# Layer 0's pass by source in a four-layer graph network: the one-hot of a batch made by one comparison on VectorE

## The reference, cut to what matters

```python
# edge_index = stack([src, dst]); row, col = src, dst;  h = relu(layernorm(x))
messages = h[col] * fsum                       # fsum: one number for each edge, from edge_weight
agg = jax.ops.segment_sum(messages, row, num_segments=x.shape[0])
out = softplus(agg @ Wi1 + bi1) @ Wi2 + bi2
out = gamma * (out - mov_mean) * rsqrt(mov_var + 1e-3) + beta
x = x + out
```

## Time and profile before

| | us |
|---|---|
| median of three runs | 8948.55 |
| lowest and highest run | 8941.01, 8954.63 |
| the profiled execution | 9018.93 |
| its span from first to last instruction | 9017.2 |
| VectorE busy in the span | 3871.8 (43%) |
| GpSimd busy | 5604.4 (62%) |
| ScalarE busy | 1730.6 (19%) |
| TensorE matmuls busy | 3603.3 (40%) |
| mean granted TensorE clock | 0.611 |

### The profile page before, as it was taken

The page is one execution under the profiler, slowest core; times in us unless marked ns, Lnnn a source line. Parts: engine busy times, 40 slices in busy tenths (PEclk is TensorE's granted clock), DMA queues, the critical chain, the costliest instruction groups (busy, mean ns, idle before and its releaser), DMA issues. The chain is left out here.

```text
span 9017.2 us, 92622 instructions
## 1 busy us (share of the span) xinstructions
PE 3603.3 (40%) x19869; PEld 3184.5 (35%) x19870; DVE 3871.8 (43%) x10252; ACT 1730.6 (19%) x2818; POOL 5604.4 (62%) x5253
## 2 busy tenths in 40 slices
PE   4000001344435734444434444426666665344433
PEld 1000001333335633333323333325565654333333
DVE  8886001222225644434464434463333336444445
ACT  3000000000004721111121111122111114111111
POOL 2788777666666456666646666645666661666665
PEclk9555555666667955555555555556666667566666
DMA  5233333222224411111221111122222231121113
GB/s 188 62 81 92 90 89 89 66 68 68 67 67 135 127 44 42 42 42 42 41 32 42 42 42 42 42 24 71 65 64 64 64 64 23 45 45 44 44 44 46
DMA packets 385196, 561.62 MB, mean 62 GB/s; under 512 B 206364, under 2 KB 242692, under 8 KB 385000
## 3 DMA queue, kind: packets, MB, share of 16 engines
q0 software_dynamic: 171520, 305.19, 15.5%
q1 hardware_dynamic: 213608, 255.67, 9.1%
HBM read 374.00 MB, written 189.03 MB: 62 GB/s over the span
## 5 line engine op out<-in xcount | busy, mean ns | idle before, releaser
L1307 POOL DMA_INDIRECT edge_buf<-node_table,ixr x1664 | 1694.1, 1018 | 1044.6 <-PEq L1040 491.7
L1307 POOL DMA_INDIRECT Y<-node_table,ixr x1664 | 1665.1, 1001 | 936.8 <-issue 492.9
L1461 PE MATMUL bank<-ident_b,Y 128*128 128x128 bf16 x2520 | 325.5, 310 | 2303.3 <-ACT Y L1423 2253.6
L409 POOL DMA_INDIRECT edge_records<-edge_buf x800 | 991.0, 1239 | 252.6 <-issue 249.5
L1203 POOL DMA_INDIRECT layer_messages<-edge_buf,ixr x832 | 869.9, 1046 | 424.4 <-issue 253.4
L1461 PEld LDWEIGHTS bank<-ident_b,Y 128*128 128x128 bf16 x2520 | 242.4, 140 | 2380.7 <-ACT Y L1423 2328.6
L1036 PE MATMUL bank<-edge_buf,Y 128*128 128x129 f32 (+2 forms) x3744 | 843.9, 400 | 13.6 <-DVE H L1057 13.6
L1057 DVE TENSOR_TENSOR ACC<-ACC,bank 128x129 f32 (+2 forms) x2080 | 604.5, 291 | 505.9 <-PE bank L1036 260.8
L1012 DVE TENSOR_TENSOR Y<-iota_row,dloc 128x1024 f32<-128x1024 f32 x420 | 516.5, 1230 | 700.6 <-PEq L1040 651.5
L1036 PE MATMUL bank<-Y 128*128 128x129 f32 (+1 forms) x3328 | 797.6, 418 | 0.5 <-DVE ACC L1057 0.3
L1397 DVE TENSOR_REDUCE pk<-bank 128x16 f32<-128x48 f32 (+1 forms) x312 | 101.2, 324 | 1564.5 <-remote 1285.3
(11 more groups left out here) (280 smaller groups left out, 5728.5 us busy)
## 6 DMA issues: line engine op xcount, KB each, us to landing
edge_buf<-edge_records SPq DMA_DIRECT2D x208, 288.0 KB
layer_messages<-ACC SPq DMA_DIRECT2D x26, 2112.0 KB
XI<-layer_messages SPq DMA_DIRECT2D x78, 528.0 KB, 3.5
edge_records<-H SPq DMA_DIRECT2D x1, 29952.0 KB
edge_buf<-node_table,ixr POOLq DMA_INDIRECT x1664
Y<-node_table,ixr POOLq DMA_INDIRECT x1664
edge_buf<-in_edge_attr_dram SPq DMA_DIRECT2D x50, 500.0 KB
edge_buf<-layer_messages SPq DMA_DIRECT2D x26, 528.0 KB, 3.5
```

The lines of the kernel that those rows point to most:

```text
L409: pool.indirect_dma_start(rec_d, bass.IndirectOffsetOnAxis(ap=ixs[h][:, j:j + 1], axis=0), rec[h][:, j, :], None).then_inc(scattered[h], 16)
L1307: pool.indirect_dma_start(ring[q][:, j, 0:w], None, table, bass.IndirectOffsetOnAxis(ap=ixr[q][:, j:j + 1], axis=0)).then_inc(rows_in[q], 16)
L1461: ins = nc.tensor.transpose(tb_[:, j * P:(j + 1) * P], ohb[h][:, j * P:(j + 1) * P], ident_b[:, :])
```

## The change

The three steps on GpSimd and ScalarE go. VectorE makes the one-hot in one instruction, a comparison of two broadcast operands with `is_equal`. In VectorE's order the comparison for batch q + 2 stands before the additions of batch q, and two of them stand ahead of all. The wait for a free one-hot buffer and the wait for the batch's rows move from GpSimd to VectorE with it. VectorE's rounds are now written out for the first and for the last one, with a hardware loop of 11 between them. The semaphores `apart` and `distance` go. SyncE and TensorE keep their programs.

```diff
-            msg_in, apart, distance, oh_ready, used = ([sem(f"{n}{q}") for q in range(deep)] for n in
-                                                       ("msg_in", "apart", "distance", "oh_ready", "used"))
+            msg_in, oh_ready, used = ([sem(f"{n}{q}") for q in range(deep)] for n in ("msg_in", "oh_ready", "used"))
...
-                @block.gpsimd
-                def _(pool):
-                    def body(i, first):
-                        for q in range(deep):
-
-                            if q >= oh_deep:
-                                pool.wait_ge(used[q - oh_deep], i + 1)
-                                pool.sem_inc(poolt, 1)
-                            elif not first:
-                                pool.wait_ge(used[q + deep - oh_deep], i)
-                                pool.sem_inc(poolt, 1)
-                            pool.wait_ge(msg_in[q], i * 16 + 16)
-                            pool.sem_inc(poolt, 1)
-                            nc.gpsimd.tensor_tensor(onehots[q], iota_row[:, :].unsqueeze(1).to_broadcast([P, G, P]),
-                                                    by_tile[q][:, :, D:D + 1].to_broadcast([P, G, P]), ALU.subtract) \
-                                .then_inc(apart[q], 1)
-                    looped(pool, rounds, body)
-
-                @block.scalar
-                def _(act):
-                    def body(i, first):
-                        for q in range(deep):
-                            act.wait_ge(apart[q], i + 1)
-                            nc.scalar.activation(onehots[q], onehots[q], ACT.Abs, bias=zero1[:, :]).then_inc(distance[q], 1)
-                            act.wait_ge(distance[q], i + 1)
-                            nc.scalar.activation(onehots[q], onehots[q], ACT.Relu, bias=one1[:, :], scale=-1.0) \
-                                .then_inc(oh_ready[q], 1)
-                    looped(act, rounds, body)
-
                 @block.vector
                 def _(dve):
 
                     nc.vector.memset(H[:, :, :], 0.0).then_inc(odd_cleared, 1)
                     dve.wait_ge(odd_cleared, 1)
-                    looped(dve, rounds, lambda i, first: [add_sums(dve, *half_of(i, q), acc_of_s, D, summed, added)
-                                                          for q in range(deep)])
+                    def make(i, q):
+                        if q >= oh_deep:
+                            dve.wait_ge(used[q - oh_deep], i + 1)
+                        elif later(i):
+                            dve.wait_ge(used[q + deep - oh_deep], i)
+                        dve.wait_ge(msg_in[q], i * 16 + 16)
+                        nc.vector.tensor_tensor(onehots[q], iota_row[:, :].unsqueeze(1).to_broadcast([P, G, P]),
+                                                by_tile[q][:, :, D:D + 1].to_broadcast([P, G, P]), ALU.is_equal) \
+                            .then_inc(oh_ready[q], 1)
+
+                    def body(i, last):
+                        for q in range(deep):
+                            if q + 2 < deep:
+                                make(i, q + 2)
+                            elif not last:
+                                make(i + 1, q + 2 - deep)
+                            add_sums(dve, *half_of(i, q), acc_of_s, D, summed, added)
+                    make(0, 0)
+                    make(0, 1)
+                    body(0, False)
+                    with dve.Fori(1, rounds - 1) as i:
+                        body(i, False)
+                    body(rounds - 1, True)
```

## The result

The changed kernel takes 8962.72 us, the median of 20 runs (8948.05 to 8991.59), the kernel before 8944.27, the median of 20 on the same chip (8919.82 to 8960.90). The ratio is 1.0026, with the interval [1.0017, 1.0035]: slower by 23 us, at least 15 and at most 31 (this is the difference of the means; the two medians lie 18.5 us apart). The profiled execution of the changed kernel took 8952.04 us, with a span of 8950.3.

A forecast was written before the change was run, and what follows sets the result against it. It took VectorE's queue, with its bare register load, as the bound. Start +1.4, first round +2.4, eleven loop rounds +29.9 and last round +0.8 made +34.5 us on 8948.55: 8983 us, range 8957 to 9006.

The forecast's parts named there:

- the queue runs ahead: Rival on VectorE: additions follow 0.21 us apart after a 1.14 us comparison, batch 2.82, +14 us, 8963 us; chance 9%.
- What goes gives nothing: 104 GpSimd subtractions and 208 ScalarE activations were already hidden, so removing them alone gains nothing; first use at the start differs.
- What the comparison hides: In VectorE's queue the register load starts with the comparison; load and three steps, 0.87 us, fit under its 1.14.
- The new waits hold nothing: Waits on VectorE for the batch's rows and for a free one-hot buffer should not hold before a comparison.
- A batch of 3.02 us: VectorE's batch after the change: 1.14 + 0.43 + 0.50 + 0.49 + 0.21 + 0.25, against 2.68 before, 0.34 more.
- Eleven rounds: +29.9: The hardware loop's 88 batches at 0.34 us more each; the turn costs 0.40 us both before and after.
- Start, first and last round: +1.4, +2.4, +0.8: Three comparisons before the first addition, +1.4 us; first round at 2.96 a batch, +2.4; last round written out, +0.8.
- The profiler as a bound: If queue steps took no time without the profiler, batches would be 2.45 before, 2.82 after, +38 us: still slower.
- The comparison takes less room: Rival on VectorE: comparison's room under 1.0 us would gain; at half of 1.14, -24 us, 8925 us; chance 5%.
- The load is not hidden: Rival in VectorE's queue: the register load waits for the comparison's end, batch 3.89 us, +126 us, 9074 us; chance 3%.
- The clock falls: Rival on TensorE: longer standstill puts every other batch at clock 0.50, mean 3.56 us, +92 us, 9040; chance 5%.
- Each operation waits until the one before has ended: Rival on VectorE: no operation starts before the pipe is empty, batch 3.8 us at least, about +116, 9065 us; chance 3%.

The follow-up runs named there:

- e8: Kernel before with VectorE's 13 rounds written out instead of a hardware loop: 8898.98 us against 8936.27, ratio 0.9961, pass 267.2 us.
- e9: Changed kernel with all 13 rounds of VectorE written out: pass 322.1 us against 320.7 with the loop; ratio 1.0042 to the kernel before.
- e4: Kernel before with one register load of 16 values for two batches instead of 8 for each: pass 8.0 us shorter, ratio 0.9991.
- e3: Changed kernel with each batch's register load moved ahead of the comparison: pass 385.7 us against 320.7; ratio 1.0112 to the kernel before.
- e2: Kernel before plus an unused comparison on VectorE ahead of each batch's additions, GpSimd and ScalarE still making one-hots: pass +30.4 us, ratio 1.0037.
- e1: Changed kernel plus a second, unused comparison of the same form for each batch: pass 438.7 us against 320.7; ratio 1.0169 to the kernel before.
- e7: Changed kernel comparing only four of a batch's eight tiles: pass 304.0 us against 320.7; ratio 1.0012 to the kernel before.
- e11: Kernel before profiled again on another chip: profiled execution 8059.92 us, nine runs' median 8063.96, pass 294.3 us against 293.7.
- e5: Changed kernel a second time, unaltered, on another chip: 8954.84 us against 8936.27 before, ratio 1.0023, pass 321.0 us.
- e10: Kernel before plus an unused comparison on VectorE ahead of each batch, one operand from PSUM, one from SBUF: pass 320.1 us, ratio 1.0043.

## Why the prediction was right

Forecast were 8983 us and a range of 8957 to 9006, with a chance of 81% for slower. It is slower, with 8962.72 us. The mechanism is the one forecast; the sum was 7.5 us too large in the pass (+34.5 against +27.0). The other 13 of the 20 us between 8983 and 8962.72 are no merit or fault of the sum: the 20 runs of before have a median 4.3 lower than the three that the forecast started from, and the two medians lie 8.5 less apart than the two passes, which is within the interval of the ratio. So the time alone proves little: 8962.72 is also what the rival "the queue runs ahead" gave (8963). What decides between the two is the trace.

- *What bounded the pass before.* "VectorE's queue is the bound" holds, and e8 shows it: with fewer register steps a batch falls to 2.43 us, and even then it is the queue that sets it. TensorE's need, which the prediction had at 2.45, is 2.33 at most. The prediction read the pace between the even additions as the queue's too. In the loop that is so, but e9 adds what it didn't see: the wait for the last but one stands just behind it, at 0.48 against 0.50. So what the queue's steps can be made to give back lies in the hole, which e4, e8 and e3 shrink or open.
- *What goes gives nothing.* Right: e2 has the addition alone at +30.4 us. The first use, at the start, is the only place where it counts.
- *What comes: 1.14 us to the first addition.* Right to 0.01 us in the trace of after, and again in e1 (1.135 for each).
- *What the comparison hides.* Right, and the core of the sum. The load starts with the comparison, e3 puts 0.63 us on each batch by moving it ahead, e7 measures load, steps and the start of the addition at 0.97 us from the comparison's start. The prediction had 0.87 for load and steps. Paid back are 0.88 us a batch; with its 0.34 for a batch the prediction had 0.80.
- *The new waits hold nothing.* Right: there is almost no idle time ahead of the comparisons (3.5 us in 78), and none to speak of is put down to DMA or to TensorE.
- *A batch of 3.02 us.* It is 2.95. Two terms were sized too large. From the last addition to the comparison are 0.20 to 0.21 us in most batches, where 0.25 was taken: the bound of 0.21 was named beside it and would have been right. From the first to the second even addition 0.41 and not 0.43. So 1.13 + 0.41 + 0.50 + 0.50 + 0.20 + 0.20 is 2.94. One of the prediction's signs of being wrong, additions closer than 0.49, was badly set: its own row of before has 0.43 for the first pair.
- *Eleven rounds: +29.9.* They are 11 x (24.11 - 22.15) = +21.6, 8.3 less than forecast and a little more than the whole error of 7.5. The round of after was forecast at 8 x 3.02 + 0.40 = 24.56, 0.45 too much, by the two terms above. The round of before was taken as 8 x 2.68 + 0.40 = 21.84 from one batch and one turn, and is 22.15 in the trace: 0.31 too little. The third batch of a round takes 2.80 there, and the last one, with the turn, 3.23, in part since its first two even additions are 0.54 us apart and not 0.43. The sum over the rounds could have been read from the trace of before; one batch read to 0.01 us and taken 88 times isn't as good.
- *Start, first and last round: +1.4, +2.4, +0.8.* From the start of the clearing to the first addition are 9.40 us against 8.14: +1.3. The first round has 24.30 against 21.24: +3.1, where 2.96 was taken for a batch written out; it is 3.04 here and 3.00 in e9. The last round has 21.74 us to its last addition against 20.64: +1.1.
- *The profiler as a bound.* Not needed, by e11.
- *The rivals.* "The comparison takes less room": no, e1. "The queue runs ahead", 0.21 for each addition: no, though its time came out; even additions stay 0.41 to 0.50 apart and a batch takes 2.95 us, not 2.82. The prediction held against it that the load and steps fill the comparison. That is true, but e9 gives a stronger reason: with fewer steps the wait for the last but one keeps the pace at 0.48 for two. "The load is not hidden": no, e3 is how that looks. "The clock falls": no, 0.99. "Each operation waits until the one before has ended": no, additions start 0.20 us behind one of 0.28, and 1.13 behind a comparison of 1.22. The Trainium skill, "VectorE: DVE Perf Modes", section "The DRAIN you can't avoid", has the next operation wait for an empty pipe, but adds that one which is not held starts earlier; the prediction weighed the first half alone, and these starts are of the second kind.

Between the pass (+27.0) and the times (+23, and +21 in e5) lie 4 to 6 us. Both intervals hold the 27, so there is nothing left that these runs could explain.

## What to carry to other kernels

Where no engine is full, look into the queue of the engine that seems to wait for another: a register load or a chain of register steps stands there as idle time "for" an engine that had long been done. An instruction put just ahead of a register load is paid back by as much of the load as it covers, so its price is its place on the engine less that cover, and the same edit (a larger load, rounds written out) can gain on one side of such a change and lose on the other. Before an engine gets more work to hide a load, try to take away what fills its queue: here, writing the rounds out gained 35 us [22, 47], and the change gave 23 away. Whether the queue is still the bound then is not told by the idle time "for PE", nor by a batch that happens to match TensorE's forecast need, but by whether the queue's last steps run through to the addition without a gap (e8).

## What was not expected of the hardware

- A register load costs by the value. 8 values take 0.596 us and 16 take 1.104 (e4), by these two sizes about 0.09 + 0.0635 for each.
- A comparison with two SBUF operands lengthens a GpSimd subtraction that starts 0.30 us before its end, from 1.91 to 2.08 us (e2). With one operand from PSUM it doesn't (e10). The Trainium skill, "SBUF — State Buffer", section "Who interferes with whom", has it so, for VectorE instructions with two SBUF inputs; these durations agree.
- An addition that waits for the last but one starts 0.20 us behind its end where two steps of the queue lie between (e9), and 0.13 where it is one (the first pair of a batch in the changed kernel, 2967.30 + 0.28 to 2967.72). So two additions of 0.28 us take 0.48 or 0.41. A comparison follows the last addition after 0.20.
- The profiled execution of before, 9018.93 us, lies 58 us above the highest of its 20 runs (8960.90). Against the trace of after most of the excess lies in the four gather stages (1308.3, 1310.0, 1316.3 and 1312.0 us, against 1292.4, 1295.0, 1301.3 and 1294.8: 63 us together) and in what stands ahead of this pass, which starts at 2803.22 instead of 2785.56. What caused it is open. A comparison of the two spans would have shown the change as a gain of 67 us.
